# Four-layer gated decoder on one Trainium2 core: squares of queries turned and added along rows, and two reordered steps of the first state-space stage

## The reference, cut to what matters

```python
x = x + tanh(g_xattn[0]) * L0_xattn(ctx, layernorm(x), ...)   # state-space scan, 16 states: stage 0
x = x + tanh(g_ffn[0])   * L0_ffn(layernorm(x), ...)          # stage 1
... L1: attention (stage 2), feed-forward (stage 3)
... L2: the same state-space scan (its scan runs beside stages 1 and 3, its gate is stage 4), feed-forward (stage 5)
x = x + tanh(g_xattn[3]) * L3_xattn(layernorm(x), ctx, ...)   # 16 heads of 128: stage 6
x = x + tanh(g_ffn[3])   * L3_ffn(layernorm(x), ...)          # quantized feed-forward: stage 7
```

```python
# state-space mixer (stage 0)
u     = silu(conv(in_proj(ctx)) + conv_b)
delta = softplus(dt_proj(x_proj(u)[:16]) + dt_proj_b)
state = state * exp(delta * A[n]) + (delta * u) * B[n]        # for each of 16 states n, along 512 positions
y     = sum over n of state_n * C[n];  y = (y + D * u) * silu(z)

# 16-head attention (stage 6)
q = rmsnorm(x @ Wq per head, gq);  k = rmsnorm(ctx @ Wk per head, gk)   # mean of squares over 128 columns
out = softmax(q @ k.T / sqrt(128)) @ v, per head;  out @ Wo
```

## Time and profile before

| | |
|---|---|
| median of three runs | 3839.43 us |
| the profiled execution | 3838.44 us, of which its span is 3836.9 us |
| TensorE / VectorE / ScalarE / GpSimd busy, share of the span | 94% / 77% / 46% / 16% |
| 0 to 768 us (stage 0): TensorE / VectorE / ScalarE busy, granted clock | 688.95 / 639.80 / 541.17 us, 0.94 |
| 2430 to 3510 us (stage 6): TensorE / VectorE / ScalarE busy, granted clock | 1048.11 / 701.43 / 505.47 us, 0.98 |

### The profile page before, as it was taken

How to read it: one execution, slowest core, us unless ns; L and a number is a source line. 1 busy time by engine, 2 the same in 40 slices (tenths; PEclk the granted TensorE clock), 3 DMA queues, 4 the chain that set the end, 5 groups by cost and what they waited for, 6 DMA issues and landing times.

```text
span 3836.9 us, 39962 instructions
## 1 busy us (share of the span) xinstructions
PE 3592.6 (94%) x12210; PEld 1966.3 (51%) x12210; DVE 2957.1 (77%) x4863; ACT 1755.1 (46%) x2739; POOL 633.0 (16%) x596
## 2 busy tenths in 40 slices
PE   8999989899999998899999999999999999999787
PEld 4556565544444444444445788554554554554343
DVE  7798988887979797889889777675575575576497
ACT  6777676633333323334443211454354354353376
POOL 1323232333433210244321000000000000000000
PEclk8999999999999999999999999999999999999898
DMA  3323232433242322443345201221121121121000
GB/s 134 113 77 121 70 132 67 170 115 143 85 167 90 134 85 71 165 162 108 121 168 194 92 22 50 93 72 49 36 72 47 34 70 52 37 72 61 1 12 33
DMA packets 90982, 344.79 MB, mean 90 GB/s; under 512 B 11808, under 2 KB 20128, under 8 KB 77504
## 3 DMA queue, kind: packets, MB, share of 16 engines
q1 hardware_dynamic: 61264, 225.86, 16.7%
q0 software_dynamic: 29552, 116.94, 9.0%
HBM read 280.36 MB, written 62.39 MB: 89 GB/s over the span
## 4 chain that ended last, share of the span: by engine, by line
PE 55%; DVE 23%; issue 11%; ACT 7%; DMA 3%; DVEq 0%; POOL 0%; ACTq 0%; POOLq 0%; SPq 0%
PE ps L1169 35%; PE ps L1557 6%; PE ps L1388 3%; PE ps L1547 3%; PE ps L1255 3%; DVE room L1720 2%; PE ps L1242 2%; PE ps L1440 2%; DVE room L1724 2%; DVE room L1728 1%; DMA room<-bc_scratch 1%; DVE room L1778 1%; DVE stat L1684 1%; ACT room L834 1%; DVE room L1733 1%
## 5 line engine op out<-in xcount | busy, mean ns | idle before, releaser
L1169 PE MATMUL ps<-lnT,room 128*128 128x512 f32 x2240 | 986.1, 596 | 20.3 <-DVE room L1929 12.0
L1169 PE MATMUL ps<-room 128*128 128x512 f32 (+2 forms) x1888 | 720.0, 537 | 47.8 <-DVE xres L2215 17.8
L1169 PEld LDWEIGHTS ps<-lnT,room 128*128 128x128 f32 x2240 | 425.8, 191 | 564.4 <-issue 529.0
L659 POOL TENSOR_TENSOR idle<-idle 128x1 f32<-128x1 f32 x268 | 455.3, 1699 | 1304.0 <-ACT room L844 483.5
L1169 PEld LDWEIGHTS ps<-room 128*128 128x128 f32 (+1 forms) x1888 | 309.9, 168 | 433.4 <-issue 319.4
L1388 PE MATMUL ps<-room 128*128 128x512 f32 x864 | 377.9, 595 | 8.4 <-DVE room L1881 8.4
L771 ACT ACTIVATE room<-room,small 128x511 f32<-128x511 f32 x256 | 163.6, 709 | 370.3 <-DVE room L1724 370.2
L1778 DVE TENSOR_TENSOR_SCAN room<-room 128x2048 f32<-128x2048 f32 x64 | 283.2, 4425 | 14.4 <-ACT room L834 9.0
L1724 DVE TENSOR_TENSOR_SCAN room<-room 128x2048 f32<-128x2048 f32 x64 | 283.4, 4428 | 5.4
L2175 DVE TENSOR_REDUCE stat<-ps 128x1 f32<-128x512 f32 x256 | 177.1, 692 | 132.0 <-PE ps L1169 131.9
L1388 PEld LDWEIGHTS ps<-room 128*128 128x128 f32 x864 | 164.2, 191 | 214.4 <-issue 207.6
(11 more groups left out here) (236 smaller groups left out, 5112.8 us busy)
## 6 DMA issues: line engine op xcount, KB each, us to landing
room<-in_ffn SPq DMA_DIRECT2D x16, 2048.0 KB, 10.7
room<-bc_scratch POOLq DMA_DIRECT2D x128, 256.0 KB, 3.6
room<-kv_stash SPq DMA_DIRECT2D x64, 512.0 KB, 3.4
kv_stash<-room POOLq DMA_DIRECT2D x96, 256.0 KB, 2.4
room<-stash POOLq DMA_DIRECT2D x24, 1024.0 KB, 5.6
room<-in_ffn SPq DMA_DIRECT2D x20, 1024.0 KB, 5.4
room<-in_ffn SPq DMA_DIRECT2D x24, 768.0 KB, 4.9
room<-in_ffn SPq DMA_DIRECT2D x12, 1536.0 KB, 8.0
```

What stands on the lines that cost most here:

```text
L659: nc.gpsimd.tensor_tensor(idle[:, :], idle[:, :], idle[:, :], ALU.add).then_inc(zeros_added, 1)
L1169: last = nc.tensor.matmul(out, lhsT, rhs, start=(i == 0), stop=(i == len(parts) - 1))
```

## The change

Three edits. In stage 0, VectorE's `softplus(front_b)` goes behind `convolve(front_a)` at state 6 (for the first three batches; the last has no such convolution). In stage 0, ScalarE makes the decay of state 15 at the head of its state 13, ahead of the four evictions of state 13, in all batches. In stage 6, the sums of squares of a head's queries are made in another way: before, four products of the squares with a column of ones (one PSUM column each); after, four transposes of the squares (128 PSUM columns each, a whole bank), a `tensor_reduce` along the rows on VectorE, a wait for it, and the addition of the epsilon from the small tile. The wait on `h_qss_used` in `normalize` goes, as VectorE has already waited for it in `take_sums`, and the link counts are adjusted.

```diff
@@ scalar, mamba, body
                     for n in range(DS):
                         act.wait_ge(scan_done, b * DS + (n + 1))
+                        if n == DS - 3:
+                            decay(n + 2)
                         if n == 1:
                             take_inproj(1, front_b, tile)
@@
-                        if n + 2 < DS:
+                        if n + 2 < DS and n != DS - 3:
                             decay(n + 2)
-                        elif not last:
+                        elif n + 2 >= DS and not last:
@@ tensor, attention3, query_sums
                     for t in range(NT):
-                        mm = product(ps[:, 1, t:t + 1], [(h_sq[h % 2][:, t * P:(t + 1) * P], ones[:, 0:1])])
+                        mm = nc.tensor.transpose(ps[:, 1, t * P:(t + 1) * P], h_sq[h % 2][:, t * P:(t + 1) * P], ident[:, :])
                     mm.then_inc(h_qss, 1)
@@ vector, mamba, body
                         if n == 6:
-                            softplus(front_b, 1)
                             if not last:
                                 dve.wait_ge(Du_summed, b + 1)
                                 convolve(front_a, 0, tile)
+                            softplus(front_b, 1)
@@ vector, attention3
                 def take_sums(b, h):
                     dve.wait_ge(h_qss, b * H + (h + 1))
-                    v.tensor_scalar(qsums, ps[:, 1, 0:NT], HD * EPS, None, ALU.add).then_inc(h_qss_used, 1)
+                    v.tensor_reduce(qsums, t3(ps[:, 1, :], NT), AX.X, ALU.add).then_inc(h_qss_used, 1)
+                    dve.wait_ge(h_qss_used, b * H + (h + 1))
+                    link(v.tensor_scalar(qsums, qsums, HD * EPS, None, ALU.add))
@@ normalize
-                    dve.wait_ge(h_qss_used, b * H + (h + 1))
                     rsqrt(roots, sums, 2 * NT, rtmp)
@@
-                KEYS = 3 + 11
+                KEYS = 1 + 3 + 11
```

## The result

| | before | changed |
|---|---|---|
| median (lowest to highest, runs) | 3841.11 us (3836.49 to 3843.57, 4) | **3785.64 us** (3780.23 to 3790.17, 4) |
| ratio, 95% interval | | 0.9855 (0.9843 to 0.9866) |
| profiled execution, span, granted clock | 3838.44, 3836.9 us, 0.971 | 3780.23, 3778.6 us, 0.973 |

The change takes 55.5 us off the median and 58.3 off the span; 62.8 was forecast, and 3775.6 us as the time. Where the gain arises is read from starts of the same scan in both traces, and in stage 6 from starts of the scaled keys. For the changed kernel: 0.3 us at state 6 of the first batch and 10.0 at state 7; 12.2, 21.6 and 34.8 at the last state of the first three batches; 36.3 at the end of stage 0, still 36.3 at the first keys of stage 6, and 59.3 at its last keys.

A forecast was written before the change was run, and what follows sets the result against it. TensorE, ScalarE and VectorE take turns in stage 0, TensorE's chain holds stage 6. 24.6+17.2+21 = 62.8 us off the profiled 3838.4 gives 3775.6 us; forecast's own range 3762 to 3792, all cases 3759 to 3804.

The forecast's parts named there:

- Edit 1: Stage 0, state 6, three batches: the convolution fills VectorE's 9.65 us wait for exp; 3 x 8.2 = 24.6 us.
- The walk: ScalarE's list at state 6, followed by row durations: evictions end 8.2 us sooner, carried to the batch's end.
- Edit 2: Stage 0, decay of state 15 sooner: 11.2 us of waits plus 6.0 at batch boundaries, 17.2 us (11.2 to 19).
- first term: VectorE's waits for the last decay, at three batch ends, nearly vanish: 11.2 of 11.4 us.
- Its second: Three batch boundaries: TensorE keeps its upper clock for transposes and passes, 2.0 us each, 6.0 us.
- TensorE now idles under 1: Batch boundary, before the next batch's scan 0: TensorE's 3.56 us idle time falls below 1 us.
- Edit 3: Stage 6 query sums: 0.35 us saved a head on TensorE, 21 us; lower bound 10.5, upper 28.5 (0.46 a head).
- the third rival: Stage 6: VectorE's keys set the head, only 0.17 us a head won, 10.5 us; 3786 us, chance 0.15.
- Stores eat edit 1: Stage 0, state 6: ScalarE waits 7.6 us for key/value stores, edit 1 gives 0.6 a batch; 3798 us, chance 0.17.
- Clock in stage 6: Twenty transposes in a row lower TensorE's clock, 2.2 us more a head, 136 us; 3912 us, chance 0.05.
- Keys set the head: Stage 6: VectorE's scaled keys limit the gain to 0.17 us a head, 10.5 us; 3786 us, chance 0.15.
- Reordering does nothing: Stage 0 held by TensorE and ScalarE alone, VectorE's waits reappear; 3828 us with the third rival; little or nothing 0.08.

The follow-up runs named there:

- the two other traces of the same stage 0: The changed kernel with one more small VectorE instruction, ahead of the scaled keys (3797.30 us) or in `take_sums` ahead of the wait for scores (3785.84 us).
- the kernel with all three moves: The changed kernel with ScalarE's stage 0 loop written out, state 6's logarithm before the key/value unit, B's state 9 row loaded before the D*u store: 3761.29 us.
- moving the row: On the changed kernel, SyncE's load of B's row for state 9 put ahead of the store of D*u: 3777.36 us, ratio 0.9829.
- two other moves: The changed kernel with ScalarE's batch loop written out and its state 6 logarithm ahead of the late key/value unit: 3774.46 us, ratio 0.9823.

## Why the prediction came out, point by point

**What bounds the kernel** held: TensorE through a head of stage 6, and engines in turn in stage 0.

**Edit 1**, forecast 24.6 us: right in mechanism, 2.1 us under. The full 9.7 to 9.8 us of VectorE's wait arrive at state 7, and 0.5 to 1.1 go by state 9 (the lead of the changed kernel in the second batch goes 9.2, 18.9, 17.8 at states 6, 7 and 9). Net it is 8.8+8.6+9.3 = 26.7, which is also the lead of the kernel with this edit alone. The walk had 8.2 a batch. The wait at state 9 was to grow to about 6 us; it is 5.80 in the second batch, though the profile puts it down to TensorE there.

**Edit 2**, forecast 17.2 us, was the part that failed. Its first term, 11.2 from VectorE's wait, is right: the steps at state 15 are 3.7, 3.4 and 3.7, 10.8 together. Its second, "I take 2.0 for each of three boundaries; the bound below is 0", came out at -3.1, -0.3 and +1.3, so -2.1 instead of +6.0 (in the two other traces of the same stage 0 -3.1, -2.2, +1.3 and -4.3, -2.8, +1.3). In all the edit gave 8.7 us, half of its forecast and under the lower bound of 11.2. Two things were wrong in it. First, "TensorE now idles under 1" holds for the transposes (0.33) but not for the sums behind them: ScalarE's loop turns just there, 3.37 and 1.21 us with nothing to wait for, and was covered before by a wait of 4.41 for the slow transposes. At the first boundary, after the idle 2.50 us, TensorE's granted clock falls again: over 225 to 240 us it is 0.89, and six passes take 4.54 us. At the second, after 1.69 us, it does not, and the same six take 2.84, which is why the loss there is small in this trace.

```profile
225.00:240.00 15.00, 11.73 (x62) 7.81 (x62) 14.71 (x7) 5.39 (x11) 0.00 (x0) 0.89 0.05 19
```

With the loop written out the term is +1.9 and +2.2 at these two boundaries, as it was sized. Second, one boundary was taken for three. At the third no loop turns, and TensorE's slow stretch was shorter already before: 7.0 us from the first transpose to the end of the sums, against 7.7 and 7.9 at the other two, and 16 transposes in 2.37 us against 3.67. There the term is 1.3 and shows only at state 7 of the last batch. A look at all three would have told them apart.

**Edit 3**, forecast 21 us, measured 23.0 (23.8 alone). The size per head was taken at 0.35 us and is 0.46, the "upper" of the text, the spacing of the eight products' weight loads: in the chain 0.35 goes with the sums themselves (0.79 against 0.44) and 0.10 more with the products behind them (2.68 against 2.58). Over the 60 intervals between keys inside the batches the gain is 27.0 us (0.45 each). The three intervals that hold a batch's end grew by 1.6, 0.4 and 2.1 us, 4.1 together, which leaves 23.0. In the kernel with all three moves they hardly change (+0.1, -0.4, +0.1) and 27.4 us are won. Whether this loss is a price of the edit stays open: such an interval takes anything from 59.5 to 62.1 us, the first one was over 61 in six of the nine traces with the edit and 59.9 in all three without it, and its cause wasn't tried.

**The sum.** 26.7+10.8-2.1 = 35.4 in stage 0; the small steps left make it 36.3. With 23.0 in stage 6 that is 59.3, and 58.3 at the end. Edits 1 and 3 were under by 2 us each, edit 2 over by 8.5; that the errors partly cancel is luck, and the forecast was 4.5 us too fast by spans. The time itself, 3775.6 us, is 10.0 under the measured median: 7.3 of it are gain that didn't come (62.8 against 55.5), the rest is that the forecast counted from a run of 3838.4 us, where the kernel before has a median of 3841.11. The measured 3785.64 lies inside the forecast's own 3762 to 3792, and also on the third rival's 3786; only stage 6, at 23.0 us and not 10.5, tells the two apart.

**Rivals.** *Stores eat edit 1*: not here (1.13 us, and for TensorE). But the text's reason against it, stores issued in gaps of VectorE's list, was only half so: one came 0.11 us ahead of a multiply, the other under it. A shift of 0.12 us brings the rival's mechanism about, as the kernel with ScalarE's loop written out shows, so that it stayed away was partly luck. *Clock in stage 6*: refuted. The Trainium skill, "TensorE: Matmul & The Clock Gate", section "PE-mode transpose", says that transposes don't engage the full clock; here 20 in a row, among products, ran at a granted clock of 1.00, 0.109 us each, and the head became shorter. The trace disagrees with that sentence for transposes among products; a run of transposes alone is in no trace here. *Keys set the head*: not yet. The load did run ahead of its pass, but the room is 0.08 us, so the margin was nearly as thin as the text had it. *Reordering does nothing*: refuted by both edits alone.

## What to carry to other kernels

When an edit removes an idle wait, look at what else lay under it: here a loop's turn on another engine, worth nothing until then, took the place of the gain. Check a term that is multiplied by a count at every one of its places. And take the size of a small gain from repeated times: two single traces put moving the row at 1 us, where the timings put it at about 10 (uncertain by 8), and it still added 8 us beside two other moves.

## What was not expected of the hardware

The turn of ScalarE's loop costs 3.37 us before the first and 1.21 us behind the first instruction of the next pass, and disappears when the loop is written out. It costs nothing where ScalarE would wait longer anyway (4.41 us in the kernel before). A one-element GpSimd instruction took 0.24 us when it started 0.11 us ahead of a VectorE multiply, 2.33 us when it started with one, and 3.96 us when it started inside a VectorE scan of 4.42 us; it ended when the multiply or the scan did. And a float32 product with a single output column costs more of TensorE than a 128-column transpose: eight passes held a head for 0.90 us (0.44+0.46), four transposes for 0.44.
